# Three layernorm pairs and the weights of two layers drawn into the blocks ahead of them

## The reference

```python
x = x + attn_a(_layernorm(x), ...)   # linear attention, 16 heads, kernel features relu(q @ rw) + eps
x = x + ffn(_layernorm(x), ...)      # two local-attention layers (n = 0, 1)
x = x + attn_b(_layernorm(x), ...)   # softmax over the key index, all rows of a sequence
x = x + ffn(_layernorm(x), ...)      # the same two layers again (n = 2, 3)

def _layernorm(x, eps=1e-05):
    return (x - mean(x)) / sqrt(var(x) + eps)

def _layer(x, wqkv, qs, ksc, wo, lg, lb, w1, b1, w2, b2):   # one layer of ffn
    h = shift_token(x)                # second half of the features from the token before
    q, k, v = split(h @ wqkv)
    q, k = rotary_xpos(l2norm(q) * qs, l2norm(k) * ksc)
    x = x + local_attention(q, k, v) @ wo           # windows of 64, looking one back
    h = layernorm(shift_token(x)) * lg + lb
    a, g = split(h @ w1 + b1)
    return x + (a * gelu(g)) @ w2 + b2
```

## Time and profile before

| | us |
|---|---|
| runs | 1784.83, 1780.13, 1783.86 |
| median | 1783.86 |
| profiled execution | 1789.27 |
| its span | 1787.5 |
| PE busy | 1688.6 (94%) |
| DVE busy | 1340.3 (75%) |
| ACT busy | 1307.9 (73%) |
| POOL busy | 1124.5 (63%) |
| granted PE clock, mean | 0.984 |

### The profile page before, as it was taken

How to read it: one execution, slowest core, us unless ns; L and a number is a source line. 1 busy time by engine, 2 the same in 40 slices (tenths; PEclk the granted TensorE clock), 3 DMA queues, 4 the chain that set the end, 5 groups by cost and what they waited for, 6 DMA issues and landing times. The chain is left out here.

```text
span 1787.5 us, 43489 instructions
## 1 busy us (share of the span) xinstructions
PE 1688.6 (94%) x15560; PEld 1096.2 (61%) x15560; DVE 1340.3 (75%) x2367; ACT 1307.9 (73%) x4472; POOL 1124.5 (63%) x1014
## 2 busy tenths in 40 slices
PE   8997899999989999998999999899999999999999
PEld 5663677775657777554344444477776556777655
DVE  5554898974778989456688886698985688898645
ACT  5444788887358888745899998688887537888863
POOL 6554899992579999603212220799996278999730
PEclk9999999999999999999799999999999999999999
DMA  2002111103011110202655551211102102110111
GB/s 69 2 2 62 25 32 25 26 20 86 13 41 29 29 26 20 63 1 40 125 93 107 87 95 34 68 28 31 26 19 55 51 1 55 26 31 20 43 30 42
DMA packets 67309, 74.90 MB, mean 42 GB/s; under 512 B 13380, under 2 KB 50968, under 8 KB 65048
## 3 DMA queue, kind: packets, MB, share of 16 engines
q1 hardware_dynamic: 67096, 72.13, 18.9%
HBM read 28.08 MB, written 10.49 MB: 22 GB/s over the span
## 5 line engine op out<-in xcount | busy, mean ns | idle before, releaser
L457 POOL TENSOR_TENSOR rsum<-pa,pb 128x512 f32<-128x512 f32 x256 | 325.7, 1294 | 67.1 <-DVE pa L373 37.7
L839 ACT ACTIVATE ffn_prob<-sc,ffn_nmax 128x128 f32<-128x128 f32 x928 | 327.5, 387 | 6.8 <-DVE ffn_nmax L756 6.8
L923 POOL TENSOR_TENSOR ffn_prob<-ffn_prob,ffn_rden 128x512 f32<-128x512 f32 x256 | 265.7, 1060 | 54.3 <-DVE ffn_rden L771 46.7
L466 POOL TENSOR_TENSOR rsum<-rsum,ffn_rnt 128x512 f32<-128x512 f32 x256 | 262.0, 1045 | 8.2 <-ACT ffn_rnt L861 5.9
L383 DVE TENSOR_TENSOR pb<-proj,ffn_tab 128x512 f32<-128x512 f32 x236 | 161.5, 685 | 84.4 <-ACT rn L427 84.1
L839 ACT ACTIVATION_READ_ACCUMULATOR ffn_prob<-sc,ffn_nmax 128x1 f32 x928 | 209.5, 226 | 0.0
L363 PE MATMUL pt<-ident,rsum 128*128 128x128 f32 x960 | 154.2, 284 | 15.1 <-POOL rsum L466 12.4
L756 DVE TENSOR_REDUCE ffn_nmax<-sc 128x4 f32<-128x512 f32 x232 | 148.5, 682 | 16.1 <-PE sc L653 13.4
L363 PEld LDWEIGHTS pt<-ident,rsum 128*128 128x128 f32 x960 | 100.8, 141 | 96.6 <-ACT ffn_ptb L847 70.5
L394 DVE TENSOR_REDUCE ffn_ss<-rn 128x16 f32<-128x1024 f32 x128 | 154.4, 1206 | 0.0
L682 PE MATMUL ob<-ffn_ptb,ffn_v 128*64 128x64 f32 (+1 forms) x3072 | 143.7, 243 | 9.1 <-issue 9.1
(11 more groups left out here) (291 smaller groups left out, 4275.7 us busy)
## 6 DMA issues: line engine op xcount, KB each, us to landing
ffn_v<-ffn_v SPq DMA_DIRECT2D x128, 128.0 KB, 2.3
column_ks<-qk_parts SPq DMA_DIRECT2D x64, 128.0 KB, 4.1
rn<-Y SPq DMA_DIRECT2D x32, 128.0 KB, 2.3
qk_parts<-column_hi SPq DMA_DIRECT2D x64, 64.0 KB, 1.6
qk_parts<-column_lo SPq DMA_DIRECT2D x64, 64.0 KB, 1.7
column_qs<-qk_parts SPq DMA_DIRECT2D x32, 128.0 KB
column_qs<-qk_parts SPq DMA_DIRECT2D x64, 64.0 KB
rn<-Y SPq DMA_DIRECT2D x32, 127.5 KB, 2.4
```

Of the source, the lines that this page charges most:

```text
L457: pool.tensor_tensor(K.sm[:, r, w], K.m1[:, r, w], K.m2[:, r, w], ALU.add).then_inc(S.f_sum, 1)
L466: pool.tensor_tensor(heads(K.sm[:, r, w]), heads(K.sm[:, r, w]), K.rnt[:, r, w * HEADS:(w + 1) * HEADS].unsqueeze(2).broadcast_to([P, HEAD ...
L839: ins = act.activation(K.prob[:, r, e, k], score_banks(i)[e][:, tokens(k)], ACT.Exp, bias=K.nmax[:, r, e, k:k + 1], accum_out=K.den[:, r, ...
L923: pool.tensor_tensor(K.prob[:, r, e], K.prob[:, r, e], K.rden[:, r, e].unsqueeze(2).broadcast_to([P, 4, P]), ALU.mult).then_inc(S.f_pn, 1)
```

## The change

The norms of pairs 0 to 2 of layers one and three (`ENTERED = 3`) are computed at the end of the block ahead, in new functions: `entry_centre` and `entry_variance` (PE), `entry_square` and `entry_inverse_root` (ACT), `entry_normal` (DVE), with the buffers lnq, lnl, lnr. Query and key weights and the rotary table are staged in the buffer pa (`query_key_stage`) and loaded by SP at the end of its list in that block (`entry_loads`), which also issues the shifted copies of pairs 0 and 1; POOL clears hs, splits and scales there (`entry_weights`). For this the split weights, the table and hs become buffers of the whole program. In the layer, pairs 3 to 7 remain, one for each filling step: centres into banks of their own, one variance bank (ss); pair 3 and pair 4 get their normals in the first step (-6 and -5 of the source, that is behind tile 0). `low_parts` of pair 0 goes from POOL to DVE. The wait of turn_tile is for 5 normals instead of 6, and values wait for 6. In all four layers two pieces of ACT's order change: in step 27 keep_queries stands ahead of keep_output, and in step 28 keep_probabilities(27) stands ahead of exponentials(28).

```diff
+def entry_loads(sp, K, n):
+    load_query_key_weights(sp, K, n)
+    sp.wait_ge(S.f_z, n // DEPTH + 1)
+    for q in range(2):
+        sp.wait_ge(S.ln_nrm, PAIRS * (n + 1) + q + 1)
+        load_shifted(sp, K, n, q)
+def entry_weights(pool, K, n):
+    pool.memset(K.hs, 0.0).then_inc(S.f_z, 1)
+    split_query_key_weights(pool, K, n)
+    scale_tables(pool, K, n)
...
+def entry_variance(pe, K, n, p):
+    pe.wait_ge(S.ln_sq, entry + p + 1)
+    if n == 0 and p >= 1:
+        pe.wait_ge(S.ln_log, entry + p)
+    if n and p >= 2:
+        pe.wait_ge(S.ln_log, entry + p - 1)
+    pe.matmul(entry_var(K, n, p)[:], K.mean_w[:], K.lnq[:, p % 2], start=True, stop=True).then_inc(S.ln_var, 1)
...
     def tensor(pe):
         if begin < 0:
-            centre(0)
-            centre(1)
-            for p in range(ahead):
-                centre(p + 2)
-                variance(p)
+            centre(ENTERED)
+            centre(ENTERED + 1)
             pe.wait_ge(S.wa_lo, 3 * n + 2)
+            query_key(pe, K, n, 0, K.proj)
...
     def vector(dve):
         if begin < 0:
-            for p in range(ahead):
-                normal(p)
-                if p in (1, 3):
-                    high_parts(dve, K, n, p // 2)
+            high_parts(dve, K, n, 0)
+            low_parts(dve, K, n, 0)
+            high_parts(dve, K, n, 1)
             dve.wait_ge(S.wa_tab, n + 1)
...
-            if due(i) is not None:
+            if due(i - 1) == ENTERED:
+                normal(ENTERED)
+            if due(i) is not None and i > FIRST:
                 normal(due(i))
...
     def scalar(act):
         if begin < 0:
-            square(0)
-            for p in range(ahead):
-                square(p + 1)
-                inverse_root(p)
+            square(ENTERED)
...
             if due(i) is not None:
                 if due(i) + 1 < PAIRS:
                     square(due(i) + 1)
+                if i == FIRST:
+                    squares(act, K, n, 0, K.proj)
                 inverse_root(due(i))
...
-            if 1 <= i <= LATE:
+            if 1 <= i <= LATE + 1:
                 keep_probabilities(i - 1)
...
-            if LATE < i <= TILES:
+            if LATE + 1 < i <= TILES:
                 keep_probabilities(i - 1)
...
-            if 1 <= i <= LATE:
+            if 1 <= i < LATE:
                 keep_output(i - 1)
             if 0 <= j - 1 < TILES:
                 keep_queries(act, K, n, j - 1, pt[0])
+            if i == LATE:
+                keep_output(i - 1)
...
     def gpsimd(pool):
         if begin < 0:
-            pool.memset(K.hs, 0.0).then_inc(S.f_z, 1)
-            split_query_key_weights(pool, K, n)
-            low_parts(pool, K, n, 0)
-            scale_tables(pool, K, n)
             split_value_weights(pool, K, n)
             low_parts(pool, K, n, 1)
...
 # linear_programs, vector
+        entry_normal(dve, K, 0, 0)
         divide(PAIRS - 1)
         residual(PAIRS - 1)
+        entry_normal(dve, K, 0, 1)
+        entry_normal(dve, K, 0, 2)
...
 # column block, tensor
             row_sums(SEQS - 1, 3, 0)
+            pe.wait_ge(S.b_ex, 32 * SEQS - 6)
+            entry_centre(pe, K, DEPTH, 2)
             row_sums(SEQS - 1, 3, 1)
+            pe.wait_ge(S.b_ex, 32 * SEQS)
+            entry_variance(pe, K, DEPTH, 0)
             turn(SEQS - 1)
+            entry_variance(pe, K, DEPTH, 1)
             spread(SEQS - 1)
+            entry_variance(pe, K, DEPTH, 2)
             project(SEQS - 1)
```

More of the change, by code:

```diff
@@ new lines, in entry_square, with entry_inverse_root @@
+def entry_square(act, K, n, p):
+    S, entry = K.s, PAIRS * (n + 1)
+    act.wait_ge(S.ln_cent, entry + p + 1)
+    if p >= 2:
+        act.wait_ge(S.ln_var, entry + p - 1)
+    act.activation(K.lnq[:, p % 2], entry_cent(K, n, p)[:], ACT.Square).then_inc(S.ln_sq, 1)
+def entry_inverse_root(act, K, n, p):
+    S, entry = K.s, PAIRS * (n + 1)
+    act.wait_ge(S.ln_var, entry + p + 1)
+    act.activation(K.lnl[:, p % 2], entry_var(K, n, p)[:], ACT.Ln, bias=K.eps[:]).then_inc(S.ln_log, 1)
+    act.wait_ge(S.ln_log, entry + p + 1)
+    act.wait_ge(S.ln_nrm, entry + max(0, p - 1))
+    act.activation(K.lnr[:, p % 2], K.lnl[:, p % 2], ACT.Exp, scale=-0.5).then_inc(S.ln_rstd, 1)
@@ L583, in sync @@
         if begin < 0:
-            load_query_key_weights(sp, K, n)
-            sp.wait_ge(S.f_z, n // DEPTH + 1)
-            for q in range(2):
-                sp.wait_ge(S.ln_nrm, entry + q + 1)
-                load_shifted(sp, K, n, q)
-                if q == 0:
-                    load_value_weights(sp, K, n)
+            load_value_weights(sp, K, n)
         load_mlp_weights(sp, K, n)
@@ L1706, in _ @@
                 load(2 * i + 3)
+            entry_loads(sp, K, DEPTH)
         @block.gpsimd
@@ L1960, in _ @@
                                                bias=B.nm[:, slot, bt:bt + 1], accum_out=B.dn[:, slot, bt:bt + 1]).then_inc(S.b_ex, 1)
+            for p in range(ENTERED):
+                entry_square(act, K, DEPTH, p)
+                if p >= 1:
+                    entry_inverse_root(act, K, DEPTH, p - 1)
+            entry_inverse_root(act, K, DEPTH, ENTERED - 1)
 class Semaphores:
```

128 lines of the change are left out of this document (92 added, 36 removed).

## The result

The changed kernel took 1764.59 us (median of four runs, 1763.04 to 1770.82), the kernel before 1782.17 beside it (1780.13 to 1784.83): a ratio of 0.991, 95% interval 0.989 to 0.993, or 17.6 us less. Two later comparisons on other chips gave 1765.22 to 1782.55 (0.990, 0.988 to 0.993) and 1767.26 to 1783.14 (0.991, 0.989 to 0.993). The forecast was 1763.5, with 20.3 us of gain. Its profiled execution took 1770.82, with a span of 1769.0, 18.5 us less than before.

What follows compares the result with a forecast made beforehand. At the entries a filling pipeline of norms was taken as the bound, not PE's steady work; gains of 8.0, 8.9 and 3.4 us made 20.3, from median 1783.86 to 1763.5 us, range 1757 to 1773.

Steps and rivals of the forecast that it cites:

- The entries: Heads of layers one and three: sin(1) 12.0 us after block start instead of 22.1, saving 10.2 and 10.1 us.
- the filling step: Steps after sin(1) in layers one and three: stay 5.1 us, with added norms fitting into DVE's 0.67 us idle.
- signs of being wrong: Block start later than 157, inverse_norms(0) waiting over 2 us for roots, filling steps over 5.3, or granted clock under 0.9.
- The linear end: End of the linear block, three norms added: layer one begins 2.2 us later, at 155.1; bounds +0.5 to +6.
- SP's copy of pair 1: Linear block's end: leaves behind normal(1), about 153.8; 1.1 us of issue ends at 155; costs nothing.
- The column end: End of the column block, three norms added: 1.2 us longer (0 to +4), layer three entered at 1115.9.
- Part four: ACT's order from step 27 in all four layers: −0.85 us per layer, −3.4 in all.
- Rival C: ACT's new order gives nothing or costs, as PE's other waits set the end: 1767 or 1768.5; chance 0.20.
- The sum: Whole kernel: 8.0 for layer one, 8.9 for layer three, 3.4 for ACT's order, 20.3 us in all.
- Rival A: Heads of layers one and three: PE's clock does not fall, about 2.4 us back per entry, 1759; chance 0.13.
- B: Norms stay serial at the block ends, which grow by 6 us instead of 2.2 and 1.2: 1774; chance 0.08.
- D: Slower: PE's clock falls later, fillings and steps behind them stay at half clock, ending at 1788; chance 0.03.

Runs made afterwards that it cites:

- e12: The changed kernel itself, measured a third time: 1767.26 us beside 1783.14 for the kernel before, ratio 0.991.
- e10: Changed kernel with column centres behind last scores, linear variance 2 ahead of last project, two unused PE products ending both blocks: 1765.35 us to 1782.35 before, ratio 0.989.
- e1: Kernel before with only the change's new ACT order in all four layers: 1780.87 us to 1780.90 before, ratio 1.000.
- e4: Changed kernel with all norms and shifted copies back at the layer heads and ACT's old order, weights still early: 1780.03 us to 1780.90 before, ratio 1.000.
- e8: Changed kernel with the column block's centres 0 and 1 moved from sequence 15 to behind the last scores: 1765.69 us to 1782.35 before, ratio 0.990.
- e5: The changed kernel itself, measured again: 1765.22 us to 1782.55 for the kernel before, ratio 0.990.
- e2: Changed kernel with ACT's old order in the tail: 1769.69 us to 1780.90 for the kernel before, ratio 0.994.
- e11: Changed kernel with ACT's old order again, beside the change on one chip: 1768.29 us, kernel before 1783.14.
- e7: Changed kernel with PE's attend ahead of project in steps 28 to 32 of all layers: 1772.76 us to 1782.55 before, ratio 0.994.
- e6: Changed kernel with two unused centring products at the end of PE's list in linear and column blocks: 1763.55 us to 1782.55 before, ratio 0.990.
- e9: Kernel before with unused centring products, three in the linear block's end and two in the column block's: 1780.00 us to 1782.35 before, ratio 0.998.

## Why the prediction was right, point by point

**The entries** were the forecast's core, and the mechanism held at each step: products wait for norms no more, sin(0) stands 4.6 us into the block (5.9 forecast; centres 3 and 4 took 2.5 us instead of 3.7, since the block began at full clock), ACT's two roots delay inverse_norms(0) and set sin(1) (t + 11.1 for t + 12.0), the filling step keeps its 5.1 us, and the norms put into it cost nothing. Entries -11.05 and -10.91 for -10.2 and -10.1. One of the signs of being wrong did show, a block start later than 157 (159.04); it is the first piece's fall of 3.56 us, and in e12, without it, layer one starts at 155.93.

**The linear end** came at +2.55 for +2.2, and by the chain as written: variance(2) at 155.62, its root at 156.68, the normal at 158.06. The normal ends at 158.75, 0.29 us ahead of the layer, as the residual did before (152.64 and 152.93). But SP's copy of pair 1 was said to cost nothing, with its issue ending 0.1 us ahead of the layer. Its issue ends 0.70 us ahead here, and where it is the last by far, in e10, 0.65: it is as late as the chain, and with the chain shortened the end did not move. The step that failed is the cover named for SP's copies; that it cost nothing here is owed to a chain just as long.

**The column end** was mis-sized: +2.53 for +1.2, and 3.9 against e1 and e4 (22.95), where the clock had not fallen in the old end. Two centres inside sequence 15 cost 1.63 us, since scores and exponentials queue behind them, and not "little"; e8 shows that elsewhere they cost as much. The other 2.3 us lie behind that, where the variances, roots, normals and SP's copies stand. SP's last issue sets the end here: the layer follows it by 0.65 us (1108.02 to 1108.67), as in e10, but follows the normal's end (1108.18) by 0.49 instead of 0.29. Net, layer one's entry brought 8.5 us (8.0 forecast) and layer three's 8.4 (8.9) by these two profiles; beside e1, whose clock had not fallen there, layer three's brought 8.4 at the entry and lost 3.9 at the end, 4.5 net.

**Part four** failed. 0.12 us a layer stands for 0.85. The step that failed is "from there ACT is the bound to the end of the layer". The exponentials of step 30 do come 0.83 us sooner, as forecast, but those of step 31 wait for the ring that starts at keep_output(27), and that had gained a copy of 0.47 and lost 0.38. Rival C (nothing, 1767) was the right one for this part.

**The sum** over the parts is 8.5 + 8.4 + 0.5 = 17.4 us, and the medians moved by 17.6. That they agree so well is in part luck, since the profile of before had a fall at layer three's head that e1 and e4 had not. The four pieces of the table above sum to 86.4 us in the mean of before, e1 and e4, and to 71.3 in that of change, e5, e12, e2 and e11; that is 15.0, with part four 15.5, for medians that moved by 17.6, 17.3 and 15.9. The profiles moved by 18.5 by chance: the change's own had the fall at 28 to 40 us (+3.56), that of before had falls which the other had not, at 732 us (-1.5), at the head of the column block (-1.9) and at 1155 us (-1.4). The forecast time, 1763.5, lies 1.1 from the measured one, because 20.3 was taken from a median of 1783.86 that came out as 1782.17 with one more run; the gain itself was 2.7 too large.

**Rival A** came in part. At both heads of the change's profile the clock was up when the block began and fell for a shorter time, and in layer one of five other kernels of its kind (e2, e7, e8, e11, e12) it did not fall at all, for 1.6 us (11.1 to 9.5). That is less than the 2.4 priced, since a fall at the new head is shorter (some 3.4 us at half clock) than the 5.07 us of the earlier trace rows. The prediction's reading that the clock "falls after 1.12 us of idle at the barrier" is wrong: it was at 0.50 from 151.3 on. The Trainium skill ("TensorE: Matmul & The Clock Gate", Part 1) has activity as what releases the throttle; the six heads of e6, e9 and e10 fit that, but with nearly the same work ahead of them the clock fell at eight heads and stayed up at six, which no run here explains.

Rivals B and D did not come: the norms' chain lies under the old one up to the last link, and the fillings ran no slower; the fall near 190 us of the kernel before costs 1.35 us where it comes, in either kernel.
